# Both pairs of key tiles added on GpSimd, denominators of two tiles, normalise on VectorE

## What is computed

```
x = x + 0.5 * ffn(layernorm(x))
x = x + attention(layernorm(x))
x = x + 0.5 * ffn(layernorm(x))

# attention: 16 heads of 64
q, k, v = split(x @ w_qkv.T)
q = q * cos + rotate_half(q) * sin + fenc      # k the same
attn = softmax(q @ k.T / 8)                     # per batch and head, 512 x 512
out = (attn @ v) @ w_out.T + b_out
```

## Time and profile before

| | |
|---|---|
| time, median of 3 runs | 1315.5 us (1313.26 to 1315.73) |
| the profiled execution | 1315.65 us, its span 1313.9 us |
| mean granted TensorE clock | 0.987 |
| busy: PE, DVE, ACT, POOL | 97%, 64%, 47%, 67% |
| attention (periods 0 to 63) | about 260 to 1107 us of the span |

### The profile page before, as it was taken

The page is one execution under the profiler, slowest core; times in us unless marked ns, Lnnn a source line. Parts: engine busy times, 40 slices in busy tenths (PEclk is TensorE's granted clock), DMA queues, the critical chain, the costliest instruction groups (busy, mean ns, idle before and its releaser), DMA issues.

```text
span 1313.9 us, 21618 instructions
## 1 busy us (share of the span) xinstructions
PE 1268.6 (97%) x7858; PEld 790.6 (60%) x7858; DVE 840.1 (64%) x1352; ACT 614.2 (47%) x917; POOL 883.0 (67%) x652
## 2 busy tenths in 40 slices
PE   5999998699999999999999999999999999999998
PEld 3666665456565656666565656565565655666665
DVE  6656646876666666666666666677786664565632
ACT  3443532255545455545545554545545444443422
POOL 0443444678797888798888888788888862443343
PEclk9999999699999999999999999999999999999999
DMA  5344040223233232323232323323232321442240
GB/s 164 129 177 125 6 130 16 48 42 70 55 66 58 54 70 50 74 50 74 49 74 50 70 54 65 59 54 70 50 74 50 73 34 18 146 137 81 66 153 17
DMA packets 118681, 95.40 MB, mean 73 GB/s; under 512 B 75760, under 2 KB 85008, under 8 KB 118320
## 3 DMA queue, kind: packets, MB, share of 16 engines
q1 hardware_dynamic: 118576, 94.01, 29.8%
HBM read 57.53 MB, written 2.88 MB: 46 GB/s over the span
## 4 chain that ended last, share of the span: by engine, by line
PE 91%; DVE 5%; issue 2%; ACT 1%; DMA 1%; POOL 0%; SPq 0%; DVEq 0%; ACTq 0%
PE banks L1028 17%; PE banks L450 16%; PE banks L1011 13%; PE banks L463 10%; PE banks L1043 7%; PE banks L987 7%; PE banks L952 6%; PE banks L1016 4%; PE banks L1052 4%; PE banks L971 3%; PE banks L994 1%; DVE neg_max L1201 1%; PE banks L412 1%; PE banks L405 1%; PE banks L476 1%
## 5 line engine op out<-in xcount | busy, mean ns | idle before, releaser
L1201 DVE TENSOR_REDUCE neg_max<-banks 128x2 f32<-128x1024 f32 x256 | 313.2, 1224 | 103.1 <-PE banks L987 96.8
L1125 ACT ACTIVATE work<-banks 128x1024 f32<-128x1024 f32 x256 | 250.2, 1025 | 166.6 <-PE banks L1016 166.6
L1303 POOL TENSOR_TENSOR turn<-turn,side_turned 128x512 f32<-128x512 f32 x128 | 160.6, 1275 | 132.4 <-DMA side_turned<-side 132.3
L1028 PE MATMUL banks<-work 128*64 128x512 f32 x1024 | 233.9, 599 | 0.0
L1297 POOL TENSOR_TENSOR turn<-turn,fenc 128x512 f32<-128x512 f32 x128 | 161.9, 1287 | 14.9 <-DVE side L1194 10.9
L1308 POOL TENSOR_TENSOR qk_l<-turn,qk_h 128x512 fp32r<-128x512 f32 x128 | 162.0, 1287 | 0.9 <-ACT qk_h L1130 0.9
L1313 POOL TENSOR_TENSOR work<-work 128x1024 f32<-128x1024 f32 x64 | 152.8, 2387 | 11.2 <-PE banks L1028 11.2
L1028 PEld LDWEIGHTS banks<-work 128*64 128x64 f32 x1024 | 67.8, 136 | 132.9 <-issue 110.1
L987 PE MATMUL banks<-qk_h 64*128 64x512 f32 x512 | 118.0, 455 | 13.2 <-DVE neg_max L1201 10.2
L796 POOL TENSOR_TENSOR turn<-turn,work 128x512 f32<-128x512 f32 x56 | 72.2, 1294 | 87.1 <-DVE turn L717 87.1
L796 POOL TENSOR_TENSOR o_raw<-o_raw,work 128x512 f32<-128x512 f32 x52 | 66.8, 1288 | 89.2 <-DVE o_raw L717 89.2
(11 more groups left out here) (169 smaller groups left out, 2364.6 us busy)
## 6 DMA issues: line engine op xcount, KB each, us to landing
work<-share SPq DMA_DIRECT2D x32, 1024.0 KB, 9.3
side_turned<-side SPq DMA_DIRECT2D x256, 128.0 KB, 3.1
rec_all<-rec_d SPq DMA_DIRECT2D x128, 128.0 KB, 3.3
x_tok<-in_x SPq DMA_DIRECT2D x8, 256.0 KB, 6.1
out<-x_tok SPq DMA_DIRECT2D x8, 256.0 KB, 9.2
work<-in_w_gate_up SPq DMA_DIRECT2D x1, 1280.0 KB, 7.8
work<-in_w_qk SPq DMA_DIRECT2D x1, 1024.0 KB, 9.5
den_d<-den_rows SPq DMA_DIRECT2D x64, 4.0 KB
```

The lines of the kernel that those rows point to most:

```text
L1028: ins = nc.tensor.matmul(O[OWN[h], :], v_all[:, kt, n * DH:(n + 1) * DH], pt[:, g % 2, kt, h * T:(h + 1) * T], start=(kt == 0), stop=(kt = ...
L1125: nc.scalar.activation(pt[:, g % 2, kt, :], S[kt].rearrange("p h q -> p (h q)"), ACT.Exp, scale=QSCALE).then_inc(s["probs"], 1)
L1201: nc.vector.tensor_reduce(neg_max[:, g % 2, qt::DH], M2, AX.X, ALU.max, negate=True).then_inc(s["maxes"], 1)
L1303: nc.gpsimd.tensor_tensor(turn[:, g % 2, part], turn[:, g % 2, part], side_turned[:, part], ALU.add).then_inc(done, 1)
```

## The change

Three things:

1. GpSimd adds both pairs of tiles: tile 1 to tile 0 behind `first_applied`, and tile 3 to tile 2 behind `o_ps` (all four tiles applied). `denominators` sums two tiles instead of three: 8 matmuls instead of 12, and waits for `second_sum`.
2. In GpSimd's period the two sums stand together between `turned_part` and `low`. Before, `normalise` stood there, and the single sum stood behind `low`.
3. `normalise` moves to VectorE, behind `reciprocals`. At the hand-over, `normalise(61)` stands at the end of attention's list (behind the routing of period 63), `normalise(62)` behind unit 4 and `normalise(63)` behind unit 9.

```diff
                 def denominators(g, p):
...
-                    pe.wait_ge(s["first_sum"], g + 1)
-                    for n, kt in enumerate((2, 3, 0)):
+                    pe.wait_ge(s["second_sum"], g + 1)
+                    for n, kt in enumerate((0, 2)):
...
-                                                       pt[:, g % 2, kt, first:first + HALF], start=(n == 0), stop=(n == 2))
+                                                       pt[:, g % 2, kt, first:first + HALF], start=(n == 0), stop=(n == 1))
...
+                def normalise(g):
+                    dve.wait_ge(rec_in[g % 2], 32 * (g // 2 + 1))
+                    dve.wait_ge(s["o_copied"], g + 1)
+                    at_least(dve, s["y_ps"], g - 1)
+                    nc.vector.tensor_tensor(o_t[:, g % 2], o_raw[:, g % 2], rec_all[:, g % 2],
+                                            ALU.mult).then_inc(s["o_ready"], 1)
...
                     if exists(p - 2):
                         reciprocals(p - 2)
+                    if exists(p - 3):
+                        normalise(p - 3)
                     norm(p, 2)
...
                     for p in PERIODS:
                         period(p)
+                    normalise(N - 3)
...
                     reciprocals(N - 1)
+                elif tail == 4:
+                    normalise(N - 2)
...
+                elif tail == 9:
+                    normalise(N - 1)
...
-                def first_sum(g):
+                def pair_sums(g):
                     pool.wait_ge(s["first_applied"], g + 1)
-                    nc.gpsimd.tensor_tensor(pt[:, g % 2, 0, :], pt[:, g % 2, 0, :], pt[:, g % 2, 1, :],
-                                            ALU.add).then_inc(s["first_sum"], 1)
...
+                    nc.gpsimd.tensor_tensor(pt[:, g % 2, 0, :], pt[:, g % 2, 0, :], pt[:, g % 2, 1, :], ALU.add)
+                    pool.wait_ge(s["o_ps"], g + 1)
+                    nc.gpsimd.tensor_tensor(pt[:, g % 2, 2, :], pt[:, g % 2, 2, :], pt[:, g % 2, 3, :],
+                                            ALU.add).then_inc(s["second_sum"], 1)
...
-                    if exists(p - 3):
-                        normalise(p - 3)
+                    if exists(p - 1):
+                        pair_sums(p - 1)
                     if exists(ahead):
                         low(ahead, K, s["k_high"])
                         low(ahead, Q, s["q_high"]).then_inc(s["low"], 1)
-                    if exists(p - 1):
-                        first_sum(p - 1)
...
-                normalise(N - 3)
-                first_sum(N - 1)
-                normalise(N - 2)
-                normalise(N - 1)
+                pair_sums(N - 1)
```

8 lines of the change are left out of this document (1 added, 7 removed).

## The result

| | before | after |
|---|---|---|
| median | 1315.62 us | 1362.04 us |
| lowest and highest of the runs | 1313.26, 1316.68 | 1360.14, 1369.0 |
| ratio after : before | | 1.0366, 95% interval 1.0348 to 1.0384 |
| span of the profiled execution | 1313.9 us | 1359.6 us |
| TensorE, VectorE, GpSimd busy | 1268.6, 840.1, 883.0 us | 1263.4, 938.6, 978.6 us |

The change costs 46 us; 23.5 were forecast, and 1362 lies 6 us above the top of the range. The sign was right, half of the amount was missing.

A forecast was written before the change was run, and what follows sets the result against it. It took the steady 13.28 us period as held by the round trip matmul, VectorE reduction, matmul, which fewer denominators do not shrink. Terms -1.5 + 2 + 12 + 3 + 8 = +23.5 on 1315.65 gave 1339 us, range 1322 to 1356.

The forecast's parts named there:

- Part 1: Denominators, twelve matmuls to eight: 0 us saved in steady periods, -1.5 us in the last periods (bounds -1 and -2).
- The wave: One of three rounds of four side-by-side denominator matmuls, 0.48 us; dropping it would leave a wait for VectorE's reduction.
- Part 2: GpSimd gains a second sum and loses normalise: 12.97 us of a 13.28 us period, not the bound, 0 us.
- rival B: GpSimd becomes the bound, its period over 13.28 us: 12 to 30 us on top, 1350 to 1369; chance 10%.
- Part 3: Normalise on VectorE in steady periods: sometimes waits for a GpSimd sum, +2 us (0 to +6).
- Part 4: Norm steps inside attention wait for GpSimd's longer sums: +12 us (+7 to +20), plus +3 in periods 0 to 3.
- Part 5: Hand-over to the second FFN: normalises stand late in VectorE's program order, delaying `project_out`; +8 us (+4 to +12).
- A: The period is TensorE's after all, every period gives back 0.48 us: 1295, or 1310 with all losses; chance 7%.
- C: No exclusion worth the name between VectorE and GpSimd; normalise fits in, small steps no worse: 1320 us; chance 7%.

The follow-up runs named there:

- (1): Kernel before with the denominators' matmuls of key tile 3 left out (eight for twelve), nothing else changed: 1313.62 us, ratio 0.9996.
- 6: Kernel before with eight denominators' matmuls, and `maxima(ahead, 1)` issued before `scores(p, 3)` instead of behind it: 1349.82 us, ratio 1.0268.
- 8: Kernel before with its twelve denominators' matmuls, and only `maxima(ahead, 1)` issued before `scores(p, 3)`: 1375.81 us, ratio 1.046.
- (9): Kernel after with all normalises back on GpSimd in their old places, both sums and eight matmuls kept: 1345.37 us, ratio 1.0239.
- (16): Kernel after with each GpSimd sum of 1024 columns cut into two of 512, everything else as it is: 1376.2 us.
- (4): Kernel after with the layer norm's small steps left out of periods 47 to 53, except the first and last step: 1334.81 us.
- (5): Kernel before with the layer norm's small steps left out of periods 47 to 53: 1313.69 us, ratio 0.9985.
- (2): Kernel before with the normalise alone moved to VectorE, at the hand-over too; one sum and twelve matmuls stay: 1331.8 us, ratio 1.0135.
- (3): Kernel after with the last three normalises (pairs 61 to 63) back on GpSimd in their old places: 1361.38 us.
- (11): Kernel after with the first `apply_v` step moved ahead of the denominators and VectorE's residual between its two reductions: 1394.81 us, ratio 1.0615.
- (12): Both sums and VectorE normalise only in periods 4 to 45 and 55 to 58, kernel before's scheme elsewhere, one `apply_v` step moved ahead of the denominators: 1343.16 us, ratio 1.0201.

## Why the prediction was half right

Of the 22 us that the sum lacks, 10.8 lie in the periods of the small steps (22.8 for 12), 4.8 at the hand-over (12.8 for 8), 3.0 in the tokens' period (nothing in the sum), 1.5 in a saving that did not come, and 2.2 in the first and the steady periods. The top of the range, 1356, is also 1.7 us less than its own high ends give (+42 on 1315.65).

**Part 1, the matmuls: the mechanism right, the credit too high.** The wave has become a wait, as the earlier trace rows said, and alone it gives nothing (1), while the order that does not hide it shows 0.39 us (6 against 8). Of the 1.5 us at the end, (1) shows 0.5: from pair 60 to pair 63 it takes 30.74 us, before 31.21. In the kernel after they are lost in the waits of the hand-over.

**Part 2, GpSimd: right.** The steady period stayed at 13.27, and no denominators wait for the second sum. An instruction that VectorE's normalise holds up loses 0.49 us where 0.62 stood. With the normalise left on it, GpSimd does bind, at 13.37 (9): the margin was as thin as forecast, and rival B would have been the case of that kernel. The move of the normalise is what paid for the second sum.

**Part 3, the steady normalise: the mechanism and the amount right, its distribution not.** +3.3 for +2. The mean of L1221 is 1.31 us where about 1.2 was forecast. But the sum had a quarter of 60 periods at about 0.15 us; in the trace four periods carry the loss, three at about 0.9 and one at 1.4, where 0.7 was named as the most. The periods with a front part were not singled out. That few at a high price come out near many at a low one is luck.

**Part 4, the small steps: this is the first step that failed, a term taken from the wrong end of its bounds.** The sum said +12, between +7 and +20, "by whether a small step can slip in right behind the normalise before GpSimd, which has been waiting, takes its turn". None did. Behind the normalise GpSimd takes the next turn with a whole sum, and then the two alternate: each linked step one GpSimd instruction. L268, L270, L276, L279, L283, L286 and L288 all show 2.2 to 2.35 us in these periods. The spread of period 47 came 12.75 us into the period, where 11.2 to 12.4 stood. Period by period (47 to 54) the excess is 5.7, 4.2, 1.7, 2.6, 3.5, 0.6, 2.2 and 2.3 us, where the upper values were 3.6, 3.9, 2.7, 2.7, 2.7, none, 2.7 and 2.7: above them in 47, 48 and 51, nearer to them than to the lower ones (0.3) in the others with steps. The upper values add up to 21.0, and not to the 20 of the sum. For what goes beyond them, 1.8 us in all and 2.1 in period 47 alone, there is a term that the prediction lacked: TensorE's clock stands at its lower level for most of the 8 us behind the stall (0.57 granted in the window above); how much of it that is was not measured apart. That the price follows the instruction's length is shown by (16), that the loss needs these steps at all by (4) and (5). The Trainium skill, "SBUF — State Buffer", section "Who interferes with whom", has the rule of the shared port with the words "Issue order, not op shape, decides who blocks". By that rule alone four linked steps wait for at most one running instruction each, as here; it does not say who is next when both are waiting, and on that the forecast's choice hung.

**Part 5, the hand-over: the order of events right to 0.1 us, its second half mis-sized.** Taken back by the 32.9 us lost until pair 62, `normalise(61)` starts at 1112.6 where 1112.7 was forecast, `project_out(61)` at 1114.1 (forecast 1114.0), the first gated product at 1115.9 (1115.9). From there the forecast let `reciprocals(62)` follow as before, at 1118.2; it came at 1121.3. It stands behind the second gated product, and that waits for TensorE (L717 at 1153.32 above; 1112.35 before). TensorE's work starts with `project_out(61)`, which the forecast itself put 5.8 us later than before (measured: 5.9); it then moved everything behind by the 5.0 of the first product. That is 0.9 of the missing 3.1 us. The other 2.2 came on the way from `project_out(61)` to that product, 6.36 us for 4.18, with four matmuls fewer. The granted clock was 0.68 there; it was 1.00 over the same work before (views by windows, after and before):

```profile
1146.00:1156.00 10.00, 9.04 (x51) 6.47 (x52) 3.22 (x9) 4.56 (x8) 0.00 (x0) 0.68 0.03 0
```
```profile
1107.00:1117.00 10.00, 10.00 (x72) 7.25 (x71) 7.97 (x30) 4.72 (x8) 0.48 (x1) 1.00 0.03 0
```

So 3.1 us of the missing 4.8 are one term taken too short, the way from the normalise to `reciprocals(62)`. From there to `reciprocals(63)` it is 10.57 us for 9.91, 0.7 more, on a way that ends with a wait for a DMA; its cause is open. `project_out(62)` takes 2.08 us for 1.16, and that gives the last 0.9. (2) and (3) show the same from outside: the move of the three normalises costs 10.0 us with one sum, and with them back on GpSimd two sums cost nothing. The 2.8 us between 10.0 and 12.8 come where both meet. 1.7 of them are the second wait for a sum in the routing chain (L685 and L687, where before one step, L681, took 2.29): in the kernel after `normalise(61)` starts 1.7 us later than in (2), near the 1.8 of the forecast.

**Not in the sum at all:** the tokens' period. Four single-input operations of FFN 2 (L723) stand in period 61. They took 3.97 us together before (VectorE of the kernel before, then VectorE, GpSimd and TensorE of the kernel after):

```profile
1070.87 3.97 DVE L723 TENSOR_SCALAR xn_odd<-x_tok,rs,shift_c 128x128 f32<-128x128 f32 x4
```
```profile
1101.12 6.34 DVE L723 TENSOR_SCALAR xn_odd<-x_tok,rs,shift_c 128x128 f32<-128x128 f32 x4
```
```profile
1104.89 2.49 POOL L1322 TENSOR_TENSOR qk_l<-turn,qk_h 128x512 fp32r<-128x512 f32 x2
```
```profile
1108.65 0.80 PE L987 MATMUL banks<-qk_h 64*128 64x512 f32 x2 [4.06 <-DVE neg_max L1201]
```

They end at 1107.46, with the second of the two `low` parts (1107.38) that follow the two sums on GpSimd, and TensorE waits 4.06 us for the reduction behind them, where it waited 1.91: +3.0 us in the stretch. With the sums cut in two, (16), that is gone, though this stretch is not steady: in (5), which has there what the kernel before has, it is 1.4 us shorter. The prediction listed the periods of the small steps and the hand-over, and left this one out.

**Not foreseen either:** the lost turn. It is not in the profiled execution, so it explains nothing of the 45.7 us. But it can be why the runs of the change spread over 9 us and those of the kernel before over 3.4, one lost turn being about 7 us; for the unprofiled runs that is only argued, here as for (16).

The rivals: A fell with (1), B with the steady period of 13.27 us. C fell too: where it said that a small step is no worse, steps of 0.16 us take 2.35.

## What to carry to other kernels

Before moving work between VectorE and GpSimd, list the small linked VectorE operations on SBUF tiles that run beside GpSimd, and charge each with one whole GpSimd instruction of the longest kind that will stand there, not with a value between two bounds. Long GpSimd instructions are as dear as their length times the number of such links, so they belong where VectorE works from PSUM. In pieces they cost each step less, but (16), with halves, was no faster: its profiled run lost 31.7 us to four lost turns. A saving on the busiest engine is worth what the wait behind it leaves: look at what the next instruction waits for before counting it.

## What the runs showed that was not expected

- **Who is next at the shared port.** As a rule a waiting VectorE instruction comes in when the running GpSimd one ends, and the two alternate. But in some executions it loses its turn, and then loses it to every GpSimd instruction queued without a pause, until GpSimd waits for something else. Of the profiled executions of the sixteen kernels six show it: three normalises in (3), one in (4), one each in (11) and (12), four in (16), two small steps in (9) of 8.81 and 7.83 us and a group of four there of 9.55. They are 7.3 to 9.9 us long, and a steady period with one of a normalise grows by 6.4 to 8.8. None shows in the kernels before and after. What decides it is open.
- **Shorter GpSimd instructions cut the wait for each turn, but did not make a lost turn shorter**: with the sums in halves it lasted 8.8 to 9.9 us.
- **Single-input steps wait, too.** A TENSOR_SCALAR of eight columns from SBUF to SBUF (L279) took 2.30 us beside a sum in the kernel after, like those with two inputs; the residual with one input in PSUM (L1228) took 0.68 us on average.
